# GpSimd multiplies two states by C in one operation, on another set of states

## The chip, the cores and the metric

The kernel runs on one core of one Trainium2 chip. The metric is the device time of one launch in microseconds. The engines are named as in the profile: PE is TensorE (matmuls), DVE is VectorE, ACT is ScalarE, POOL is GpSimd, SP is SyncE (it issues the DMAs here).

## What is computed

One transformer-like layer on x of shape 4 x 512 x 512 (four batches `b`, 512 steps of time, 512 features): a layer norm, then a selective state-space block and a gated feed-forward block on the same normed input, both added to x. What matters here is the state-space part, with 1024 channels and N = 16 states per channel:

```
dA  = exp(A * dt)                 # per channel, state and step
dBu = (dt * B) * hs
h   = dA_t * h + dBu_t            # a recurrence over the 512 steps
y   = sum over the 16 states of h * C_t
y   = (y + hs * D) * silu(gate)
out = y @ Wout^T
```

The feed-forward part is `gelu(x8 @ W0) * (x8 @ W1)`, rounded to fp8 and multiplied with a third matrix. It is cut into pieces and run beside the recurrence.

## The kernel before

Stage A (the first 220 us of the execution) norms the input, computes the projections and writes dt, dt * hs and hs of every unit to memory. Stage B, the rest, is what the change touches. It works through 32 **units**: for each batch `b` the eight blocks `k` = 0 to 7 of 128 channels. A tile is 128 channels by 512 steps, 512 fp32 numbers in a partition. In each unit, for each state n = 0 to 15:

- ACT makes `da` (line 994, `exp`) into one of four PSUM tiles (`SLOTS`), which it takes up again for state n + 4. It may do so when the state that lies there is left (`state_left`, line 803): for a state whose product is DVE's, when the product is made; for a state whose product is GpSimd's, already when the scan is done, because that scan wrote its result elsewhere.
- GpSimd makes `dbu` for two states at a time (line 833, 1024 numbers in a partition), into a ring of eight states (`DBUS`).
- DVE runs the recurrence as one scan (line 1095) from `da` and `dbu`. For a state of its own the result overwrites `da`, and DVE multiplies it by C (`times_c`, line 1070) behind the next state's scan, into a ring of eight. For a **pooled** state the result goes to the ring `hp` in SBUF, and GpSimd multiplies it by C there (line 1058).
- PE transposes each product into the sum of the unit (line 1222), states of DVE in step n, pooled state m in step m + `PE_LAG`, but at the latest in step 15.

Before the change the pooled states are 1, 4, 7, 9 and 12 in every unit, `hp` has five slots, and `PE_LAG` is 4. GpSimd's order is written out by hand (`body`, line 1042): in step n first `dbu` of states n and n + 1 if n is even, then the product of state n - 3 if that is pooled. Every wait is on its own engine's in-order queue, so an operation that waits holds all behind it.

Three further pieces lie in the loop. In the **feed-forward units** k = 1 to 5, ACT runs a gelu (line 972, with a table load on either side) between `da` of states 0 and 1, and DVE makes two bf16 operations (lines 1108 and 1111, together `act8`) behind the scan of state 4; GpSimd waits for their end before the product of the pooled state `PORT_GIVEN`. In every unit but the first, ACT copies the sum of the unit before (`y_t`, line 961) and makes its silu (line 982, again between two table loads) just before `da` of state 6 (`SWITCH`), and DVE multiplies the two (line 1078) behind the scan of state 7 (`GATED`). Units k = 0, 6 and 7 have no gelu and no `act8`; they are called the plain units below.

SP loads C and B of the next batch in unit k = 7, group by group, each when the products that read the old one are made.

Of the kernel before, what the change touches and what calls it, by code (L numbers as in the profile page):

```python
# [18 lines left out]
ALU = mybir.AluOpType  # L19
# [9 lines left out]
KU = DI // P  # L29
# [12 lines left out]
NS = 2  # L42
# [5 lines left out]
DTS = 4  # L48
SWITCH, GATED, GELU, SKIP = 6, 7, 1, 12
DBUS = 8  # L50
FIVE, FOUR = (1, 4, 7, 9, 12), (1, 4, 8, 12)
POOLED = (FIVE,) * KU
POOL_LAG, PE_LAG = 3, 4
HPS, PRODS = 5, 8
EARLY = 6


# [25 lines left out]

OWN = tuple(tuple(n for n in range(N) if n not in POOLED[k]) for k in range(KU))
PROD, HP = Ring(OWN, PRODS), Ring(POOLED, HPS)
ADDED = [{n: [m for m in POOLED[k] if min(m + PE_LAG, N - 1) == n] for n in range(N)} for k in range(KU)]

# [11 lines left out]
MADE = {group[:2]: k for k in OUT_A_LIN for group in OUT_A_LIN[k]}  # L99
OUT_A_COPIED = {(5, 8): 0, (5, 11): 1, (6, 8): 2, (6, 13): 3}  # L100
LIN_COPIED = {(5, 14): 0, (6, 1): 1, (6, 15): 2, (7, 14): 3}
GELU_USED, PORT_GIVEN = 4, 4
BACK = 4

MORE = {("out_a", 2): 5, ("out_a", 3): 6}
# [609 lines left out]
def stage_b(nc, xT, win_gate, wout, outT, ident, neg_a, skip, ahead, dram, sem, handed):  # L715
# [10 lines left out]
    with ExitStack() as ctx:  # L726
        def sb(name, shape, dt=F32):
            return ctx.enter_context(nc.sbuf_tensor(name, shape, dt))
# [7 lines left out]
        hp = sb("hp", [P, HPS, L])  # L736
# [4 lines left out]
        c_all = [c_head[:, g * NS:(g + 1) * NS, :] for g in range(G_AHEAD)]  # L741
# [32 lines left out]
        hp_ready, hp_used = sem("hp_ready"), sem("hp_used")  # L774
# [28 lines left out]
        def state_left(b, k, n):  # L803

            if n in POOLED[k]:
                return scanned, (b * KU + k) * N + n + 1
            return prod_ready, PROD.count(b, k, n)

        def unit_loads(b, k):

            return b * (16 * KU // 2) + 16 * (k // 2) + 16

        def run_units(eng, body):

            for k in range(HT):
                body(0, k, True)
            for b in range(B - 1):
                for k in range(HT, KU):
                    body(b, k, False)
                for k in range(HT):  # L820
                    body(b + 1, k, False)
            for k in range(HT, KU):
                body(B - 1, k, False)
# [6 lines left out]
        def two_states(slot, n):  # L830

            twice = unit[:, slot, 1:2, :].broadcast_to([P, NS, L])
            return nc.gpsimd.tensor_tensor(dbu[:, n % DBUS:n % DBUS + NS, :], twice, b_all[n // NS], ALU.mult)  # L833
# [193 lines left out]
        def gpsimd_b(pool):  # L1027
            def make_dbu(b, k, n, opening):
                u = b * KU + k
                if n == 0:  # L1030
                    pool.wait_ge(unit_loaded[k % 2], unit_loads(b, k))
                if k == 0 and n % NS == 0:

                    if n >= G_AHEAD * NS:
                        pool.wait_ge(b_loaded[n // NS], b * 16 + 16)
                    elif not opening:
                        pool.wait_ge(b_loaded[n // NS], b * 16)
                if not (opening and k == 0 and n < DBUS):
                    pool.wait_ge(scanned, u * N + n + NS - DBUS)
                two_states(k % 2, n).then_inc(dbu_ready, NS)  # L1040

            def body(b, k, opening):
                u = b * KU + k
                for n in range(N):

                    if n % NS == 0 and not (opening and k == 0 and n < EARLY):
                        make_dbu(b, k, n, opening)
                    m = n - POOL_LAG
                    if m in POOLED[k]:

                        tile = hp[:, HP.slot(k, m), :]
                        if 1 <= k <= FFN_UNITS and m == PORT_GIVEN:
                            pool.wait_ge(act8_ready, b * FFN_UNITS + k)
                            pool.sem_inc(waited, 1)
                        pool.wait_ge(scanned, u * N + m + 1)
                        if k == 0 and (m % NS == 0 or m - 1 not in POOLED[k]):
                            pool.wait_ge(c_loaded[m // NS], b * 16 + 16)
                        nc.gpsimd.tensor_tensor(tile, tile, c_all[m // NS][:, m % NS, :], ALU.mult).then_inc(hp_ready, 1)  # L1058

            run_units(pool, body)  # L1060

        def vector_b(dve):
# [260 lines left out]
```

## Time and profile before

| | us |
|---|---|
| median of 3 runs | 1091.9 (1091.71 to 1093.25) |
| the profiled execution | 1091.34 |
| its span, first to last instruction | 1089.6 |
| PE, DVE, ACT, POOL busy | 921.8, 1028.2, 799.4, 892.0 |

The span is cut into groups of instructions by line and engine, each with its count, mean duration and the idle time of its engine just before it, and what ended that. A timeline gives single instructions with their start; where rows of a kind follow each other they are merged (x2). Durations of neighbours on DVE, ACT and POOL overlap by a little, so what one costs a full engine is read from the distance of two starts, called the pitch here.

### The profile page before, as it was taken

Reading aid. Unit: us, or ns where it says so; the run is one execution under the profiler, and the core shown is the slowest. Engines: PE = TensorE matmul, PEld = TensorE weight load, DVE = VectorE, ACT = ScalarE, POOL = GpSimd, SP = SyncE. Lnnn points to the kernel's source line nnn. Section 1 sums busy time; section 2 is a strip of 40 time slices with the busy share of each in tenths; the row PEclk is TensorE's granted clock in tenths of the full one; section 3 lists DMA queues with packets and bytes.
Section 4 is the critical chain, followed back from the end, with each engine's and each line's share of the span. In section 5 each row is a group of like instructions: output and inputs, shape, how many; then the busy total and the mean of one; then the engine's idle time right before and its main releaser. Section 6 shows DMA issues by size and latency. Waiting matters only on the chain.

```text
span 1089.6 us, 14626 instructions
## 1 busy us (share of the span) xinstructions
PE 921.8 (85%) x4328; PEld 568.2 (52%) x4328; DVE 1028.2 (94%) x1214; ACT 799.4 (73%) x1134; POOL 892.0 (82%) x496
## 2 busy tenths in 40 slices
PE   3988889777777997998889969987998798879998
PEld 3746566444444554555545545554555555545554
DVE  7979898799999999999999999999999999999996
ACT  3777877677778665888886668888866688888662
POOL 4444525798888899988888999988889988888993
PEclk9999999979999999899899989999899899989999
DMA  8686878992111218342212183321212922212101
GB/s 280 197 273 226 308 209 326 370 371 86 54 59 37 69 61 282 143 144 70 67 33 84 56 305 122 128 78 59 82 45 75 343 90 92 78 59 78 39 0 39
DMA packets 53156, 150.23 MB, mean 138 GB/s; under 512 B 5728, under 2 KB 14048, under 8 KB 50016
## 3 DMA queue, kind: packets, MB, share of 16 engines
q1 hardware_dynamic: 53088, 149.41, 39.7%
q8 instruction: 32, 0.52, 0.2%
q14 instruction: 36, 0.29, 0.1%
HBM read 111.37 MB, written 38.01 MB: 137 GB/s over the span
## 4 chain that ended last, share of the span: by engine, by line
DVE 36%; issue 28%; ACT 17%; PE 13%; POOL 5%; DVEq 1%; DMA 1%; POOLq 0%
DVE da L1095 14%; DVE prod L1070 10%; DVE hp L1095 7%; ACT da L994 4%; PE yT L1222 3%; POOL dt_du L371 2%; ACT gate_bf L972 2%; PE mm L1131 2%; ACT L973 2%; ACT L972 2%; DVE y L1078 2%; ACT L983 2%; ACT L982 2%; POOL hs_lo L366 1%; DVE gate_bf L1108 1%
## 5 line engine op out<-in xcount | busy, mean ns | idle before, releaser
L994 ACT ACTIVATE da<-unit,neg_a 128x512 f32<-128x512 f32 x512 | 339.9, 684 | 201.8 <-DVE prod L1070 200.4
L833 POOL TENSOR_TENSOR dbu<-unit,b_head 128x1024 f32<-128x1024 f32 x192 | 449.0, 2362 | 0.0
L1095 DVE TENSOR_TENSOR_SCAN da<-da,dbu 128x512 f32<-128x512 f32 x352 | 418.0, 1219 | 1.3
L1222 PE MATMUL yT<-ident,prod 128*128 128x128 f32 x1408 | 228.8, 292 | 106.8 <-DVE prod L1070 106.4
L1222 PEld LDWEIGHTS yT<-ident,prod 128*128 128x128 f32 x1408 | 172.2, 148 | 235.1 <-DVE prod L1070 187.7
L1058 POOL TENSOR_TENSOR hp<-hp,c_head 128x512 f32<-128x512 f32 x128 | 162.9, 1273 | 67.2 <-DVE act L1111 62.4
L1095 DVE TENSOR_TENSOR_SCAN hp<-da,dbu 128x512 f32<-128x512 f32 x160 | 193.7, 1211 | 9.5 <-ACT da L994 9.5
L1070 DVE TENSOR_TENSOR prod<-da,c_head 128x512 f32<-128x512 f32 x256 | 171.7, 671 | 0.0
L1171 PE MATMUL mm<-xn_b,w_sb 128*128 128x512 fp8e4 x512 | 145.9, 417 | 8.2 <-ACT gate_bf L1004 6.6
L833 POOL TENSOR_TENSOR dbu<-unit,b_all 128x1024 f32<-128x1024 f32 x64 | 151.1, 2362 | 0.0
L1183 PE MATMUL mm<-xnT_b,wgate 128*128 128x512 f32 x256 | 130.3, 607 | 2.2 <-ACT gate_bf L1004 2.1
L1131 PE MATMUL mm<-y,wout_sb 128*128 128x512 f32 x242 | 114.6, 593 | 0.8 <-DVE y L1078 0.8
L1222 PE MATMUL yT<-ident,hp 128*128 128x128 f32 x640 | 100.8, 282 | 0.0
L366 POOL TENSOR_TENSOR hs_lo<-hs,hs_hi 128x512 fp32r<-128x512 f32 x32 | 44.7, 1401 | 60.3 <-ACT hs_hi L552 60.3
L1171 PEld LDWEIGHTS mm<-xn_b,w_sb 128*128 128x128 fp8e4 x512 | 51.3, 106 | 66.8 <-issue 37.2
L1222 PEld LDWEIGHTS yT<-ident,hp 128*128 128x128 f32 x640 | 79.0, 147 | 0.0
L432 DVE SCALAR_TENSOR_TENSOR conv<-proj,cols_sb,conv 128x511 f32<-128x511 f32 (+2 forms) x96 | 71.0, 747 | 4.6 <-ACT conv L534 2.4
L371 POOL TENSOR_TENSOR dt_du<-dt_du,hs 128x512 f32<-128x512 f32 x32 | 41.1, 1285 | 39.1 <-DVE dt_du L490 38.3
L599 PE MATMUL proj<-xnT_lo,win_hi 128*128 128x512 f32 x128 | 58.2, 455 | 9.3 <-issue 3.7
L1131 PEld LDWEIGHTS mm<-y,wout_sb 128*128 128x128 f32 x242 | 43.5, 191 | 42.9 <-issue 41.9
L1070 DVE TENSOR_TENSOR prod<-da,c_all 128x512 f32<-128x512 f32 x96 | 65.0, 678 | 0.0
L1192 PE MATMUL mm<-act,w_sb 128*128 128x512 fp8e4 x256 | 61.8, 379 | 0.0
(117 smaller groups left out, 1263.7 us busy)
## 6 DMA issues: line engine op xcount, KB each, us to landing
unit<-unit_d SPq DMA_DIRECT2D x32, 768.0 KB, 4.4
unit_d<-dt_du SPq DMA_DIRECT2D x32, 512.0 KB, 2.7
wf<-in_wffn SPq DMA_DIRECT2D x12, 1024.0 KB, 6.5
c_head<-bc_d SPq DMA_DIRECT2D x24, 512.0 KB, 5.1
b_head<-bc_d SPq DMA_DIRECT2D x18, 512.0 KB, 5.3
unit_d<-hs SPq DMA_DIRECT2D x32, 256.0 KB, 6.6
w_sb<-w_d SPq DMA_DIRECT2D x64, 128.0 KB, 4.3
wgate<-in_win_gate SPq DMA_DIRECT2D x32, 256.0 KB, 2.7
```

The costliest lines, as they stand in the source:

```text
L371: nc.gpsimd.tensor_tensor(dt_du[:, k % DTS, 1, :], dt_du[:, k % DTS, 0, :], hs[:, k, :], ALU.mult).then_inc(du_ready, 1)
L432: ins = nc.vector.scalar_tensor_tensor(out=conv[:, k % 2, back:L], in0=proj[k % 3][:, 0:L - back], scalar=cols_sb[:, k, C_TAP + TAPS - 1 - ...
L833: return nc.gpsimd.tensor_tensor(dbu[:, n % DBUS:n % DBUS + NS, :], twice, b_all[n // NS], ALU.mult)
L994: nc.scalar.activation(da[n % SLOTS][:, :], unit[:, k % 2, 0, :], ACT.Exp, scale=neg_a[:, k, n:n + 1]).then_inc(da_ready, 1)
L1058: nc.gpsimd.tensor_tensor(tile, tile, c_all[m // NS][:, m % NS, :], ALU.mult).then_inc(hp_ready, 1)
L1070: nc.vector.tensor_tensor(prod[:, slot, :], da[n % SLOTS][:, :], c_all[n // NS][:, n % NS, :], ALU.mult).then_inc(prod_ready, 1)
L1095: nc.vector.tensor_tensor_scan(state, da[n % SLOTS][:, :], dbu[:, n % DBUS, :], 0.0, ALU.mult, ALU.add).then_inc(scanned, 1)
L1131: return nc.tensor.matmul(bank[:, :], wout_sb[:, c, h * P:(h + 1) * P], y2[:, c, :], start=(c == first), stop=(c == last))
L1171: ins = nc.tensor.matmul(bank[:, :], wffn[:, k % 2, j, f, s, :].bitcast(FP8), xn8[:, f, :].bitcast(FP8), start=(f == 0), stop=(f == HT - 1))
L1183: ins = nc.tensor.matmul(bank[:, :], wgate[:, k % 2, c * P:(c + 1) * P], xnT[:, c, :], start=(c == 0), stop=(c == 3))
L1192: ins = nc.tensor.matmul(bank[:, :], wlin[:, i, h * P:(h + 1) * P].bitcast(FP8), act8[:, i, :].bitcast(FP8), start=(i == 0), stop=(i == HI ...
L1222: ins = nc.tensor.matmul(yT[k % 2][:, t * P:(t + 1) * P], product[:, t * P:(t + 1) * P], ident[:, :], start=False, stop=last, is_transpose ...
```

## The change

The pooled states change from (1, 4, 7, 9, 12) in every unit to (2, 3, 6, 7, 10, 11) in units k = 0, 2, 4, 6, 7 and (2, 3, 10, 11) in units k = 1, 3, 5. GpSimd makes the product of a pair in one operation of 1024 numbers, when the scan of the second is done, in step 6, 10 and 14. `hp` has six slots, pooled states join the sum five steps later instead of four, and the wait for `act8` stands before the pair (2, 3).

```diff
-FIVE, FOUR = (1, 4, 7, 9, 12), (1, 4, 8, 12)
-POOLED = (FIVE,) * KU
-POOL_LAG, PE_LAG = 3, 4
-HPS, PRODS = 5, 8
+SIX, FOUR = (2, 3, 6, 7, 10, 11), (2, 3, 10, 11)
+POOLED = (SIX, FOUR, SIX, FOUR, SIX, FOUR, SIX, SIX)
+POOL_LAG, PE_LAG = 3, 5
+HPS, PRODS = 6, 8
...
-GELU_USED, PORT_GIVEN = 4, 4
+GELU_USED, PORT_GIVEN = 4, 3
...
                     m = n - POOL_LAG
-                    if m in POOLED[k]:
-
-                        tile = hp[:, HP.slot(k, m), :]
+                    if m in POOLED[k] and m % NS == NS - 1:
+
+                        slot = HP.slot(k, m - 1)
+                        tiles = hp[:, slot:slot + NS, :]
...
                         pool.wait_ge(scanned, u * N + m + 1)
-                        if k == 0 and (m % NS == 0 or m - 1 not in POOLED[k]):
+                        if k == 0:
                             pool.wait_ge(c_loaded[m // NS], b * 16 + 16)
-                        nc.gpsimd.tensor_tensor(tile, tile, c_all[m // NS][:, m % NS, :], ALU.mult).then_inc(hp_ready, 1)
+                        nc.gpsimd.tensor_tensor(tiles, tiles, c_all[m // NS], ALU.mult).then_inc(hp_ready, NS)
```

What it moves on GpSimd, in unit k = 2, from the product behind the wait for `act8` to the first `dbu` of unit k = 3. Before:

```order
L1058 TENSOR_TENSOR hp<-hp,c_head 128x512 [waits act8_ready,scanned]
L833 TENSOR_TENSOR dbu<-unit,b_head 128x1024 [waits scanned] x2
L1058 TENSOR_TENSOR hp<-hp,c_head 128x512 [waits scanned]
L833 TENSOR_TENSOR dbu<-unit,b_all6 128x1024 [waits scanned]
L1058 TENSOR_TENSOR hp<-hp,c_head 128x512 [waits scanned]
L833 TENSOR_TENSOR dbu<-unit,b_all7 128x1024 [waits scanned]
L1058 TENSOR_TENSOR hp<-hp,c_all6 128x512 [waits scanned]
L833 TENSOR_TENSOR dbu<-unit,b_head 128x1024 [waits scanned,unit_loaded1]
```

Now (`b_all6` is B of states 12 and 13, `b_all7` of 14 and 15):

```order
L1059 TENSOR_TENSOR hp<-hp,c_head 128x1024 [waits act8_ready,scanned]
L833 TENSOR_TENSOR dbu<-unit,b_head 128x1024 [waits scanned] x2
L1059 TENSOR_TENSOR hp<-hp,c_head 128x1024 [waits scanned]
L833 TENSOR_TENSOR dbu<-unit,b_all6 128x1024 [waits scanned]
L833 TENSOR_TENSOR dbu<-unit,b_all7 128x1024 [waits scanned]
L1059 TENSOR_TENSOR hp<-hp,c_head 128x1024 [waits scanned]
```

Four single products between the wait and the next unit's `dbu` have become three pairs, and two pairs instead of two singles stand ahead of `dbu` of states 12 and 13.

On ACT, in unit k = 7 (plain), from `da` of state 0 to `da` of state 8. Each row is an `exp`, its wait tells by what its PSUM tile comes free. Before:

```order
L994 ACTIVATE da0<-unit,neg_a 128x512 [waits scanned,unit_loaded1]
L994 ACTIVATE da1<-unit,neg_a 128x512 [waits prod_ready]
L994 ACTIVATE da2<-unit,neg_a 128x512 [waits prod_ready]
L994 ACTIVATE da3<-unit,neg_a 128x512 [waits prod_ready]
L994 ACTIVATE da0<-unit,neg_a 128x512 [waits prod_ready]
L994 ACTIVATE da1<-unit,neg_a 128x512 [waits scanned]
L961 ACTIVATE y_t<-yT0 128x512 [waits hp_used]
L982 ACT_TABLE_LOAD [waits y2_ready]
L982 ACTIVATE sg<-mm1 128x512 [waits gate_mm]
L983 ACT_TABLE_LOAD
L994 ACTIVATE da2<-unit,neg_a 128x512 [waits prod_ready]
```

Now:

```order
L994 ACTIVATE da<-unit,neg_a 128x512 [waits prod_ready,unit_loaded1]
L994 ACTIVATE da<-unit,neg_a 128x512 [waits prod_ready] x5
L961 ACTIVATE y_t<-yT 128x512 [waits hp_used]
L982 ACT_TABLE_LOAD [waits y2_ready]
L982 ACTIVATE sg<-mm 128x512 [waits gate_mm]
L983 ACT_TABLE_LOAD
L994 ACTIVATE da<-unit,neg_a 128x512 [waits scanned] x2
```

`da` of state 0 and of state 5 now wait for a product of DVE (states 12 and 1 are no longer pooled), and `da` of states 6 and 7 only for a scan.

## Rows read from the trace of the kernel before

**Rows 1.** The page: the span, and each engine's busy time and instructions

```profile
span 1089.6 us, 14626 instructions
PE 921.8 (85%) x4328; PEld 568.2 (52%) x4328; DVE 1028.2 (94%) x1214; ACT 799.4 (73%) x1134; POOL 892.0 (82%) x496
```

**Rows 2.** Groups by line: out<-in, count | busy, mean ns | idle before, releaser

```profile
L833 POOL TENSOR_TENSOR dbu<-unit,b_head 128x1024 f32<-128x1024 f32 x192 | 449.0, 2362 | 0.0
L1095 DVE TENSOR_TENSOR_SCAN da<-da,dbu 128x512 f32<-128x512 f32 x352 | 418.0, 1219 | 1.3
L1058 POOL TENSOR_TENSOR hp<-hp,c_head 128x512 f32<-128x512 f32 x128 | 162.9, 1273 | 67.2 <-DVE act L1111 62.4
L1070 DVE TENSOR_TENSOR prod<-da,c_head 128x512 f32<-128x512 f32 x256 | 171.7, 671 | 0.0
```

**Rows 3.** Waits of the whole span: who waited for whom, us, times, longest

```profile
ACT da L994 <- DVE prod L1070: 200.4, 217, 2.4
POOL hp L1058 <- DVE act L1111: 62.4, 20, 3.8
DVE hp L1095 <- ACT da L994: 9.5, 20, 0.8
```

**Rows 4.** Timeline of POOL, a feed-forward unit: start, us, line, count

```profile
524.22 1.26 POOL L1058 TENSOR_TENSOR hp<-hp,c_head 128x512 f32<-128x512 f32 x1 [2.81 <-DVE act L1111]
525.45 4.66 POOL L833 TENSOR_TENSOR dbu<-unit,b_head 128x1024 f32<-128x1024 f32 x2
530.06 1.27 POOL L1058 TENSOR_TENSOR hp<-hp,c_head 128x512 f32<-128x512 f32 x1
...
534.83 2.36 POOL L833 TENSOR_TENSOR dbu<-unit,b_all 128x1024 f32<-128x1024 f32 x1
537.15 1.27 POOL L1058 TENSOR_TENSOR hp<-hp,c_all 128x512 f32<-128x512 f32 x1
538.38 7.00 POOL L833 TENSOR_TENSOR dbu<-unit,b_head 128x1024 f32<-128x1024 f32 x3
```

**Rows 5.** Timeline of DVE, same unit: scans of states 5, 6, 12, 0

```profile
523.96 2.34 DVE L1095 TENSOR_TENSOR_SCAN da<-da,dbu 128x512 f32<-128x512 f32 x2
526.21 0.68 DVE L1070 TENSOR_TENSOR prod<-da,c_head 128x512 f32<-128x512 f32 x1
526.80 1.21 DVE L1095 TENSOR_TENSOR_SCAN hp<-da,dbu 128x512 f32<-128x512 f32 x1
...
528.50 0.68 DVE L1078 TENSOR_TENSOR y<-yT,sg 128x512 f32<-128x512 f32 x1
529.10 1.22 DVE L1095 TENSOR_TENSOR_SCAN da<-da,dbu 128x512 f32<-128x512 f32 x1
...
534.76 1.22 DVE L1095 TENSOR_TENSOR_SCAN hp<-da,dbu 128x512 f32<-128x512 f32 x1
...
541.02 1.22 DVE L1095 TENSOR_TENSOR_SCAN da<-da,dbu 128x512 f32<-128x512 f32 x1
```

**Rows 6.** Timeline of ACT, start of the feed-forward unit before: gelu ahead of state 1

```profile
510.19 0.68 ACT L994 ACTIVATE da<-unit,neg_a 128x512 f32<-128x512 f32 x1
510.89 1.28 ACT L972 ACT_TABLE_LOAD   x1
```

**Rows 7.** Timeline of DVE, the same stretch: product of 11, product of 15, scan of 1

```profile
508.38 0.67 DVE L1070 TENSOR_TENSOR prod<-da,c_head 128x512 f32<-128x512 f32 x1
...
514.64 0.68 DVE L1070 TENSOR_TENSOR prod<-da,c_all 128x512 f32<-128x512 f32 x1
515.71 1.22 DVE L1095 TENSOR_TENSOR_SCAN hp<-da,dbu 128x512 f32<-128x512 f32 x1 [0.39 <-ACT da L994]
```

**Rows 8.** Timeline of ACT, a plain unit: states 4 and 5, `y_t`, states 6 to 8

```profile
600.54 1.30 ACT L994 ACTIVATE da<-unit,neg_a 128x512 f32<-128x512 f32 x2 [1.02 <-DVE prod L1070]
601.78 0.57 ACT L961 ACTIVATE y_t<-yT 128x512 f32<-128x512 f32 x1
...
605.58 1.91 ACT L994 ACTIVATE da<-unit,neg_a 128x512 f32<-128x512 f32 x3
```

**Rows 9.** Timeline of DVE, the same plain unit: scan 1, scans 5 and 6, product of 5

```profile
598.71 1.22 DVE L1095 TENSOR_TENSOR_SCAN hp<-da,dbu 128x512 f32<-128x512 f32 x1
...
604.97 2.57 DVE L1095 TENSOR_TENSOR_SCAN da<-da,dbu 128x512 f32<-128x512 f32 x2
607.45 0.67 DVE L1070 TENSOR_TENSOR prod<-da,c_head 128x512 f32<-128x512 f32 x1
...
623.98 1.21 DVE L1095 TENSOR_TENSOR_SCAN hp<-da,dbu 128x512 f32<-128x512 f32 x1
```

## The prediction, made before the changed kernel was run

> **What bounds the kernel now.** I read four views: the busy shares, the groups by line, the waits, and then the timelines of the three engines that feed each other. The busy shares put DVE first with 94% of the span [rows 1]. The groups say that in stage B it is nearly without gaps: 1.3 us idle ahead of 352 scans, none ahead of its products [rows 2]. The waits complete it: ACT waits 200.4 us for DVE's products, so ACT is mostly early; GpSimd's one large wait, 62.4 us in 20 pieces, is for `act8` in the feed-forward units; and DVE itself waits 9.5 us, 20 times, for ACT [rows 3]. So an operation taken from DVE shortens the kernel, but only while `da` and `dbu` still arrive in time. How much room they have is what the change spends, and only the timelines show it.
>
> Pitches, from distances of starts: two scans take 526.21 - 523.96 = 2.25, so 1.125 each; a DVE product 526.80 - 526.21 = 0.59; the gated product 529.10 - 528.50 = 0.60 [rows 5]. On GpSimd two `dbu` take 530.06 - 525.45 = 4.61, so 2.31 each, and a single product 538.38 - 537.15 = 1.23 [rows 4].
>
> **Products moved off DVE.** Before, 5 pooled states in 32 units, 160. Now (5 x 6 + 3 x 4) x 4 = 168. DVE makes 8 products fewer: 8 x 0.59 = **-4.7 us**. This is all that the change can give directly.
>
> **The price of a pair on GpSimd.** The trace has none. Its nearest row is `dbu`, a product of the same 1024 numbers in a partition: pitch 2.31 [rows 4]. From above, two singles bound it: 2.46. From below, 1.23 for one half and 2.31 for both leave 1.08 per half, so 2.16 without any fixed part; a lower price would need a faster rate per number than either form shows. I take 2.31. GpSimd's products then cost 84 x 2.31 = 194 us against 160 x 1.23 = 197: almost nothing is saved there, while the work comes in lumps.
>
> **Lumps ahead of `dbu`, in the units k = 2 and 4.** Call A the start of scan 5, right behind `act8`. GpSimd starts again at A + 0.26 (524.22 against 523.96), and from there works without a gap [rows 4, 5]. Before, `dbu` of states 14, 15 ended at 534.83 + 2.36 = 537.19, and that of states 0, 1 of the next unit at 538.38 + 2.36 = 540.74, where the scan of 0 began at 541.02: only 0.28 to spare [rows 4, 5]. Now, with pair (2, 3), `dbu` 8, `dbu` 10 and pair (6, 7) ahead of it, `dbu` 12 starts at A + 0.26 + 4 x 2.31 = A + 9.50 and ends at A + 11.86. DVE has the same number of products in between as before, so it wants scan 12 at A + 10.80 (534.76) [rows 5]. With 0.04 for the signal it begins at A + 11.90: a stall of 1.10. `dbu` 0 of the next unit is the eighth operation: it ends at A + 0.26 + 7 x 2.31 + 2.36 = A + 18.79; DVE wants it at A + 17.06 (541.02), plus 1.10 already lost, 18.16, and gets it at 18.83: a further 0.67. Together 1.77 in 2 units of 4 batches, 8 x 1.77 = **+14.2 us**. With pairs at 2.46 three pairs add 0.45, so 2.22 and +17.8; at 2.16 it is 1.32 and +10.6.
>
> In the units k = 1, 3, 5 two pairs (4.62) replace five singles and DVE has two products more than in the others: `dbu` 12 ends at A + 9.55, `dbu` 0 after pair (10, 11) at about A + 16.9, before DVE wants them (A + 12 and A + 18.2). No stall. The wait for `act8` now stands one product earlier in the queue, with `dbu` 8 behind it as before; `dbu` 6 lies ahead of it in both.
>
> **Gelu ahead of state 1.** ACT makes `da` 0, then two table loads and the gelu, then `da` 1. From the start of `da` 0 to scan 1: 515.71 - 510.19 = 5.52 [rows 6, 7]. DVE would have begun scan 1 at 514.64 + 0.59 = 515.23, so it loses 0.48; in unit k = 5, whose gelu is longer by 0.43, 0.91. That is 4 x (4 x 0.48 + 0.91) = 11.3 us now, of which the waits show 9.5 as idle [rows 3]. `da` 0 used to wait for scan 12 only. Now state 12 is DVE's, and `da` 0 waits for its product, which ends 0.67 after its start; signal 0.04; so scan 1 cannot start before 0.67 + 0.04 + 5.52 = 6.23 after the start of product 12. DVE by itself takes 3 scans and 4 products, 5.74. The loss is 0.50 (k = 5: 0.93). Behind the units k = 2 and 4 the stall of 0.67 at scan 0 already covers it: nothing is left at k = 3, 0.26 at k = 5. After: 4 x (3 x 0.50 + 0.26) = 7.0, so **-4.3 us**.
>
> **`y_t` and silu ahead of state 6.** In a plain unit `da` 4 and 5 start at 600.54, right behind product 0, because state 1 is pooled and its tile is free. `y_t` follows at 601.78, `da` 6 at 605.58 [rows 8]. Scan 6 starts at 607.45 - 1.125 = 606.33, 0.75 after that; the pair of scans takes 2.57 where it takes 2.34 elsewhere, a loss of 0.23 [rows 5, 9]. Now `da` 5 waits for product 1. With s for the start of scan 1 (598.71 in the row [rows 9]), product 1 starts at s + 1.125 + 0.59 + 1.125 = s + 2.84 and ends at s + 3.51. `da` 5 starts at s + 3.55, `y_t` 0.62 later, `da` 6 another 3.80 later (605.58 - 601.78), scan 6 another 0.75 later: s + 8.72. DVE wants scan 6 after five scans and products 0, 1 and 4: s + 7.40. Loss 1.32 instead of 0.23, in 3 plain units of 4 batches less the very first unit, 11 x 1.09 = **+12.0 us**. In feed-forward units `act8` gives ACT 2 us more before scan 6, so nothing is lost there. With this wait in it, DVE takes 18.0 + 10 x 0.59 + 0.60 + 1.32 = 25.8 for a plain unit; GpSimd needs 11 x 2.31 = 25.4, so it stays just behind the cover and costs nothing more.
>
> **Edges.** In the first unit GpSimd comes late from stage A and there is no silu to slow DVE: working the chain as above from the first scan gives 1.1 of stalls, less the 0.5 of gelu that they cover, **+0.6**. At the end two pooled states join the sum behind product 15 instead of one, 4 transposes of some 0.11 more; but PE works through a backlog there. I take **+0.2** (0 to 0.4). The ring of six holds one unit's states, and PE empties it in the same unit: nothing. The C loads in k = 7 wait about 2 us longer for the pair (10, 11); their readers come 10 us later and more: nothing.
>
> **Sum.** -4.7 + 14.2 - 4.3 + 12.0 + 0.6 + 0.2 = +18.0 on the profiled execution's 1091.34 gives 1109.3. The median of the runs lies 0.56 above that execution: 1109.9, say **1110.0 us**. With a pair at 2.16 it is 1106, at 2.46 about 1114.
>
> **A rule against the change.** The groups show 1273 ns for a product on GpSimd and 671 on DVE [rows 2]. The Trainium skill, page GPSIMD Engine Reference, section Engine selection, says to keep elementwise work on VectorE, GpSimd being about twice as slow with two inputs; the trace agrees, with 1.9. By that rule alone the eight moved states would add 8 x 1.16 of GpSimd time, which the pairing gives back, and the sum would be near no change.
>
> **The rivals.** First, **the fine pieces of lateness are absorbed** and only the busy sum of the fullest engine counts: faster. The ring of `dbu` is eight states deep; if GpSimd were ahead by more than 1.8 us when it passes the wait for `act8`, neither lump would reach DVE, and if `y_t` were not behind `da` 5, nor would the other. That is -4.7 on 1091.9: 1087.2. It speaks for it that GpSimd waits 62.4 us [rows 3]; against it that this wait is for DVE itself, so it cannot be used to run ahead, and the order of ACT is fixed in the code. It decides at scan 12: if `dbu` 12 is there by A + 10.8, which needs pairs of at most 1.78.
>
> Second, **only ACT's wait comes**, GpSimd is in time: -4.7 + 12.0 + 0.7 (gelu lost in full again) + 0.2 = +8: 1100.
>
> Third, **only GpSimd's lumps come**. Without the loss at state 6 (1.32 each), the plain units are GpSimd's: 25.4 against DVE's 24.5, some 0.9 in each after a first 0.3, about 2.2 a batch. -4.7 + 14.2 - 4.3 - 2.5 + 8 + 0.8: 1103.
>
> Fourth, **GpSimd's operations become dearer** or run into DVE's two bf16 operations. In the rows GpSimd is idle while these run [rows 3]. Now `dbu` 6 of the next unit ends at A + 0.26 + 10 x 2.31 + 2.36 = A + 25.7, and line 1108 begins at about A + 26.2: 0.5 to spare. If they met, up to one `dbu` (2.36) in 8 units would be at stake: 1112 to 1129. The page Advanced Engine Details and Errata of the Trainium skill, section VectorE Performance Modes, says that the second SBUF port is shared and that GpSimd and 2-port DVE instructions block each other; no run here shows its price.
>
> **How the numbers follow.** Forecast as worked out (1105 to 1115) 0.69; only ACT 0.08; only GpSimd 0.07; dearer 0.09; absorbed 0.05; a loss and gain that cancel within 0.2% 0.02. The range from 1100 to 1116 takes in the forecast, most of the second and third and a little of the fourth, about 0.84. Faster by over 0.2% 0.05, within 0.2% (2.2 us, about what a measurement of this kernel can tell from no change) 0.02, slower 0.93.
>
> **What the profile after will show.** The pair's group, 84 long, mean near 2360 ns. DVE idle behind GpSimd's `dbu`, twice in each of 8 units, about 1.0 and 0.6; no such wait in the page now. DVE waits for `da` at scan 6 of 11 plain units, about 1.2 idle each; the waits for `da` at scan 1 in about 16 units, 0.4 each. DVE products 344, 5 us less busy. The prediction is wrong if `dbu` 12 is ready before scan 12 in units k = 2 and 4, or if `da` 6 is ready at s + 7.4 in plain units.

## The result and the profile after

The changed kernel takes **1113.4 us** (median of 4 runs, 1112.5 to 1114.7) against 1092.6 for the kernel before beside it: a ratio of 1.0191, with a 95% interval of 1.0178 to 1.0204. It is 20.9 us slower. The forecast was 1110.0, in a range of 1100 to 1116.

The profiled execution took 1114.72, with a span of 1112.9. Of the 23.3 us between the two spans, 2.1 lie in stage A, which the change does not touch (the first scan starts at 222.5 instead of 220.4; over the eight experiments below it lies between 220.6 and 222.7). Stage B is 21.2 us longer. Where the text below gives the time of stage B in a trace, it runs from the first scan to the end of the span.

The page of the changed kernel: the busy line answers to [rows 1], the groups to [rows 2].

```profile
span 1112.9 us, 14588 instructions
...
PE 918.3 (83%) x4318; PEld 565.7 (51%) x4328; DVE 1023.0 (92%) x1206; ACT 800.7 (72%) x1134; POOL 891.7 (80%) x420
...
L1096 DVE TENSOR_TENSOR_SCAN da<-da,dbu 128x512 f32<-128x512 f32 x344 | 411.9, 1214 | 20.9 <-POOL dbu L833 13.5
...
L1059 POOL TENSOR_TENSOR hp<-hp,c_head 128x1024 f32<-128x1024 f32 x84 | 198.1, 2358 | 89.4 <-DVE act L1112 78.5
L1096 DVE TENSOR_TENSOR_SCAN hp<-da,dbu 128x512 f32<-128x512 f32 x168 | 203.2, 1210 | 13.6 <-ACT da L994 13.6
```

DVE has less to do (1023.0 against 1028.2) and is idle more. Ahead of its scans it stood idle for 10.8 us before (1.3 + 9.5); now it is 20.9 + 13.6 = 34.5. GpSimd is as busy as before (891.7 against 892.0): the loss does not lie in how much it does, but in when. The waits say behind whom, and in how many places (who waited for whom, us in total, times, longest), as in [rows 3]:

```profile
ACT da L994 <- DVE prod L1071: 212.4, 233, 2.6
POOL hp L1059 <- DVE act L1112: 78.5, 20, 4.7
...
DVE hp L1096 <- ACT da L994: 13.6, 11, 1.2
DVE da L1096 <- POOL dbu L833: 13.5, 17, 1.1
...
DVE da L1096 <- ACT da L994: 7.1, 16, 1.1
```

The last three are the result. Eleven waits of 1.24 us for `da`: the plain units. Waits for GpSimd's `dbu`, which the kernel before did not have at all: 15 of the 17 come from the units k = 2 and 4 (one at scan 12, one at scan 0 of the unit behind), two from the first unit of all. And 16 waits for `da` ahead of a scan of DVE's own states: 15 are the gelu's (20 before), the sixteenth, of 1.14, is a lump of a unit k = 4 that the profile puts down to ACT.

How one of the lumps looks. DVE, then GpSimd, in a unit k = 2 (start, us, line; A, the start of scan 5, is 284.62), to be held against [rows 4, 5]:

```profile
284.62 1.22 DVE L1096 TENSOR_TENSOR_SCAN da<-da,dbu 128x512 f32<-128x512 f32 x1
...
296.67 2.35 DVE L1096 TENSOR_TENSOR_SCAN da<-da,dbu 128x512 f32<-128x512 f32 x2 [1.15 <-POOL dbu L833]
...
303.60 1.23 DVE L1096 TENSOR_TENSOR_SCAN da<-da,dbu 128x512 f32<-128x512 f32 x1 [0.58 <-POOL dbu L833]
```

```profile
284.94 2.35 POOL L1059 TENSOR_TENSOR hp<-hp,c_head 128x1024 f32<-128x1024 f32 x1 [4.65 <-DVE act L1112]
287.25 4.67 POOL L833 TENSOR_TENSOR dbu<-unit,b_head 128x1024 f32<-128x1024 f32 x2
291.88 2.38 POOL L1059 TENSOR_TENSOR hp<-hp,c_head 128x1024 f32<-128x1024 f32 x1
294.20 4.67 POOL L833 TENSOR_TENSOR dbu<-unit,b_all 128x1024 f32<-128x1024 f32 x2
298.84 2.35 POOL L1059 TENSOR_TENSOR hp<-hp,c_head 128x1024 f32<-128x1024 f32 x1
301.14 6.99 POOL L833 TENSOR_TENSOR dbu<-unit,b_head 128x1024 f32<-128x1024 f32 x3
```

From the end of the wait GpSimd runs without a gap. `dbu` of states 12 and 13 starts at 294.20 = A + 9.58 and ends 2.36 later, at 296.56; scan 12 starts at 296.67 = A + 12.05 instead of A + 10.8. The eighth operation, `dbu` of state 0, starts at 301.14, and scan 0 waits for it once more.

The plain unit, to be held against [rows 8, 9]: ACT, then DVE (scan 1 is at 635.63 = s):

```profile
639.17 0.69 ACT L994 ACTIVATE da<-unit,neg_a 128x512 f32<-128x512 f32 x1 [1.02 <-DVE prod L1071]
639.80 0.58 ACT L961 ACTIVATE y_t<-yT 128x512 f32<-128x512 f32 x1
```

```profile
635.63 1.22 DVE L1096 TENSOR_TENSOR_SCAN da<-da,dbu 128x512 f32<-128x512 f32 x1
...
638.48 0.66 DVE L1071 TENSOR_TENSOR prod<-da,c_head 128x512 f32<-128x512 f32 x1
...
644.33 1.22 DVE L1096 TENSOR_TENSOR_SCAN hp<-da,dbu 128x512 f32<-128x512 f32 x1 [1.24 <-ACT da L994]
```

`da` of state 5 starts behind product 1 (638.48 + 0.66), at s + 3.54; before it started together with `da` 4. `y_t` follows at s + 4.17, and scan 6 at s + 8.70.

### The profile page after: what moved, and what is told of

Read it like the earlier page. It is cut to its first block and busy times, and to the rows that moved or that the text cites. A ratio compares the mean times of both kernels' runs of the same rounds, so it can differ in the third digit from the quotient of the medians.

```text
span 1112.9 us, 14588 instructions
## 1 busy us (share of the span) xinstructions
PE 918.3 (83%) x4318; PEld 565.7 (51%) x4328; DVE 1023.0 (92%) x1206; ACT 800.7 (72%) x1134; POOL 891.7 (80%) x420
## 5 line engine op out<-in xcount | busy, mean ns | idle before, releaser
L994 ACT ACTIVATE da<-unit,neg_a 128x512 f32<-128x512 f32 x512 | 343.6, 686 | 214.4 <-DVE prod L1071 212.4
L1096 DVE TENSOR_TENSOR_SCAN da<-da,dbu 128x512 f32<-128x512 f32 x344 | 411.9, 1214 | 20.9 <-POOL dbu L833 13.5
L1223 PE MATMUL yT<-ident,prod 128*128 128x128 f32 x1376 | 225.6, 292 | 134.4 <-DVE prod L1071 133.6
L1223 PEld LDWEIGHTS yT<-ident,prod 128*128 128x128 f32 x1376 | 166.6, 149 | 271.3 <-DVE prod L1071 237.9
L1059 POOL TENSOR_TENSOR hp<-hp,c_head 128x1024 f32<-128x1024 f32 x84 | 198.1, 2358 | 89.4 <-DVE act L1112 78.5
L1096 DVE TENSOR_TENSOR_SCAN hp<-da,dbu 128x512 f32<-128x512 f32 x168 | 203.2, 1210 | 13.6 <-ACT da L994 13.6
L1172 PE MATMUL mm<-xn_b,w_sb 128*128 128x512 fp8e4 x512 | 143.6, 411 | 8.4 <-ACT gate_bf L1004 4.7
L1071 DVE TENSOR_TENSOR prod<-da,c_head 128x512 f32<-128x512 f32 x216 | 144.3, 668 | 0.0
L1223 PEld LDWEIGHTS yT<-ident,hp 128*128 128x128 f32 x672 | 81.6, 145 | 9.8 <-issue 4.2
L1071 DVE TENSOR_TENSOR prod<-da,c_all 128x512 f32<-128x512 f32 x128 | 85.8, 671 | 0.0
```

The source lines that it names most:

```text
L994: nc.scalar.activation(da[n % SLOTS][:, :], unit[:, k % 2, 0, :], ACT.Exp, scale=neg_a[:, k, n:n + 1]).then_inc(da_ready, 1)
L1059: nc.gpsimd.tensor_tensor(tiles, tiles, c_all[m // NS], ALU.mult).then_inc(hp_ready, NS)
L1071: nc.vector.tensor_tensor(prod[:, slot, :], da[n % SLOTS][:, :], c_all[n // NS][:, n % NS, :], ALU.mult).then_inc(prod_ready, 1)
L1096: nc.vector.tensor_tensor_scan(state, da[n % SLOTS][:, :], dbu[:, n % DBUS, :], 0.0, ALU.mult, ALU.add).then_inc(scanned, 1)
L1172: ins = nc.tensor.matmul(bank[:, :], wffn[:, k % 2, j, f, s, :].bitcast(FP8), xn8[:, f, :].bitcast(FP8), start=(f == 0), stop=(f == HT - 1))
L1223: ins = nc.tensor.matmul(yT[k % 2][:, t * P:(t + 1) * P], product[:, t * P:(t + 1) * P], ident[:, :], start=False, stop=last, is_transpose ...
```

## The experiments

All runs are compared with the kernel before on the same chip. The theory has two parts: (1) in the units k = 2 and 4 GpSimd has more work behind the wait for `act8` than DVE gives it time for; (2) in the plain units ACT's block of `y_t`, silu and two table loads (3.8 us) is held up by product 1.

**The silu two states later.** Changed kernel, with

```diff
-SWITCH, GATED, GELU, SKIP = 6, 7, 1, 12
+SWITCH, GATED, GELU, SKIP = 8, 7, 1, 12
```

> The changed kernel with one number altered: ACT copies y_t and makes the silu ahead of da of state 8 instead of state 6 (SWITCH 6 to 8). There the four states in front are 3 to 7, of which 6 and 7 find their tiles free by a scan alone. Theory (ACT's block of 3.8 us is held by product 1, which delays da 6): the 11 idles of 1.24 us ahead of scan 6 in plain units go, each worth 1.34, so -14.7; but that wait covered GpSimd, which needs 25.4 us for a plain unit with three pairs where DVE then needs 24.5, so DVE idles behind dbu there instead, about 2.2 us a batch, +8: 1106 to 1107 us. Rival A (GpSimd has room in plain units): 1098 to 1099. Rival B (ACT is late in general, the place of its block does not matter): 1113, with the idle time at another scan.

Measured: 1107.4 us (ratio 1.0140, 1.0123 to 1.0157), 6.0 faster than the changed kernel (6.9 in stage B of the two traces). The 11 idles of 1.24 ahead of scan 6 are gone, and DVE's wait for `dbu` has grown from 13.5 us in 17 places to 19.1 in 28:

```profile
DVE da L1096 <- POOL dbu L833: 19.1, 28, 1.1
...
DVE da L1096 <- ACT da L994: 5.6, 16, 0.5
```

A plain unit of this run, where GpSimd now sets the pace (DVE's scan of state 0, and GpSimd's `dbu` for it, which ends at 679.78 + 2.36 = 682.14):

```profile
682.25 1.23 DVE L1096 TENSOR_TENSOR_SCAN da<-da,dbu 128x512 f32<-128x512 f32 x1 [0.58 <-POOL dbu L833]
```

```profile
679.78 4.68 POOL L833 TENSOR_TENSOR dbu<-unit,b_head 128x1024 f32<-128x1024 f32 x2
```

Part (2) holds: the place of the block costs 11 x 1.34 = 14.7 us. Less than half of it came back. The larger part of the rest was cover for GpSimd, which in a unit with three pairs is itself slower than DVE: ten new idles behind `dbu` in and right behind the plain units, 3.9 us, and four of 0.25 at scan 12 of k = 7, where `dbu` and `da` come within 0.1 us of each other. A smaller part is the edit's own price, which I had not asked for: `y_t` two states later makes PE's sum late, and DVE stands idle for 0.53 ahead of the gated product in the four units k = 6. The other way, the new idles cover the gelu's waits of three units k = 1.

**The wait for `act8` one pair later.** Changed kernel, with

```diff
-GELU_USED, PORT_GIVEN = 4, 3
+GELU_USED, PORT_GIVEN = 4, 7
```

> The changed kernel with one number altered: GpSimd waits for act8 before the pair (6, 7) instead of (2, 3) (PORT_GIVEN 3 to 7). Units k = 1, 3, 5 have no such pair, so they have no wait. Pair (2, 3) can start when scan 3 is done, about 3.2 us earlier, while DVE makes its two bf16 operations. Theory (the stalls of 1.15 and 0.6 us behind dbu in k = 2 and 4 come of the work queued behind that wait): both go, -15.3, and the gelu wait that they covered at k = 3 and 5 comes back, +4.6: 1102 to 1104 us. Rival (sharing with DVE): DVE's two bf16 operations, 0.94 and 0.96 us now, grow in all 20 feed-forward units, by up to the rest of a GpSimd operation, 2.36: at 1 us each it eats the gain, at 2 us the kernel is slower than 1113.

Measured: 1169.7 us (ratio 1.0714, 1.0695 to 1.0734), 56 slower than the changed kernel. The waits behind `dbu` did go, from 13.5 us to 1.1. That does not test part (1), since DVE itself became 3.2 us slower in each of these units, which alone gives GpSimd time; the run with four pooled states below does. The rival came: each of the two operations stayed within its limit of 2.36, but both pay in every unit. The groups of the changed kernel, then of this run:

```profile
L1112 DVE TENSOR_SCALAR act<-gate_bf 128x1536 fp8e4<-128x1536 bf16 (+1 forms) x20 | 20.3, 1013 | 3.6 <-DVE gate_bf L1109 3.6
L1109 DVE TENSOR_TENSOR gate_bf<-gate_bf,up_bf 128x1536 bf16<-128x1536 bf16 (+1 forms) x20 | 19.8, 991 | 0.0
```

```profile
L1112 DVE TENSOR_SCALAR act<-gate_bf 128x1536 fp8e4<-128x1536 bf16 (+1 forms) x20 | 57.9, 2894 | 3.6 <-DVE gate_bf L1109 3.6
L1109 DVE TENSOR_TENSOR gate_bf<-gate_bf,up_bf 128x1536 bf16<-128x1536 bf16 (+1 forms) x20 | 46.8, 2342 | 0.0
```

The two bf16 operations grew by 37.6 + 27.0 = 64.6 us. DVE's fp32 products, one of whose inputs lies in PSUM, did not grow (666 ns against 668): in this trace the 274 that lie wholly beside a busy GpSimd take 667 ns, the 37 with GpSimd idle 662.

**Both edits.** Changed kernel, with `SWITCH` at 8 and `PORT_GIVEN` at 7.

> The two edits of e1 and e2 together: y_t and silu ahead of state 8, act8 wait before the pair (6, 7). If both causes are right and separate, the gains add: -6.7 and -10.7 on 1113.4, so about 1096 us, with DVE's idle time then behind dbu in the plain units and at gelu's da 1. If the bf16 operations of DVE suffer beside GpSimd, more by what e2 shows.

Measured: 1174.6 us (ratio 1.0762, 1.0740 to 1.0783). The 1096 that I expected were without the price that the run above shows; here the two operations grew by (61.6 - 19.8) + (52.5 - 20.3) = 74.0 us, which makes 1170. It has one thing more to show. In unit k = 1 of three batches line 1109 took 7.2 us (longest 7191 ns) instead of 0.94. DVE, then GpSimd:

```profile
485.46 7.17 DVE L1109 TENSOR_TENSOR gate_bf<-gate_bf,up_bf 128x1536 bf16<-128x1536 bf16 x1
492.80 0.96 DVE L1112 TENSOR_SCALAR act<-gate_bf 128x1536 fp8e4<-128x1536 bf16 x1 [0.16 <-DVE gate_bf L1109]
```

```profile
484.87 2.34 POOL L1059 TENSOR_TENSOR hp<-hp,c_head 128x1024 f32<-128x1024 f32 x1
487.18 4.64 POOL L833 TENSOR_TENSOR dbu<-unit,b_head 128x1024 f32<-128x1024 f32 x2
495.04 2.36 POOL L833 TENSOR_TENSOR dbu<-unit,b_all 128x1024 f32<-128x1024 f32 x1 [3.22 <-DVE da L1096]
```

DVE's operation, started in the middle of the pair, did not end when the pair ended, but 0.81 us after the last of three operations that GpSimd ran back to back (487.18 + 4.64 = 491.82). GpSimd was then idle itself, waiting for a scan of DVE. The operation behind it ran with GpSimd idle and took its plain 0.96.

**Each product by itself, in step m + 3.** Changed kernel, with

```diff
-                    if m in POOLED[k] and m % NS == NS - 1:
-
-                        slot = HP.slot(k, m - 1)
-                        tiles = hp[:, slot:slot + NS, :]
+                    if m in POOLED[k]:
+                        tile = hp[:, HP.slot(k, m), :]
...
-                        if k == 0:
+                        if k == 0 and m % NS == 0:
...
-                        nc.gpsimd.tensor_tensor(tiles, tiles, c_all[m // NS], ALU.mult).then_inc(hp_ready, NS)
+                        nc.gpsimd.tensor_tensor(tile, tile, c_all[m // NS][:, m % NS, :], ALU.mult).then_inc(hp_ready, 1)
```

> The changed kernel's sets of states, ring and lag, but each product by itself again (512 numbers, each as soon as its own scan is done, in step m + 3). Theory (what hurts in k = 2 and 4 is how much work stands behind the wait for act8, and a pair puts state 2's half there too): the product of state 2 now goes ahead of the wait, five singles of 1.23 stand behind it (6.15) where three pairs did (6.93), so the two stalls together shrink from 1.9 to 1.1 in 8 units: -6.5, though GpSimd's own work grows by 84 x 0.15 = 12.6 us. The 11 waits for da at scan 6 stay as they are. 1106 to 1108 us. Rival (the pairing is what pays, and the loss comes from the choice of states alone): slower than 1113, up to 1126 if all of the 12.6 us reaches DVE.

Measured: 1126.4 us (ratio 1.0312, 1.0294 to 1.0330). The expectation failed, though the part that it was about did not: DVE's wait for `dbu` fell from 13.5 to 7.2 us. The time is that of the rival named there, that the pairing is what pays, but not by its cause, as this run and the next show. I had not asked what else the product of state 2 is ahead of. It now stands before `dbu` of state 6, and pushes that into DVE's first bf16 operation:

```profile
L1107 DVE TENSOR_TENSOR gate_bf<-gate_bf,up_bf 128x1536 bf16<-128x1536 bf16 (+1 forms) x20 | 35.7, 1784 | 0.0
```

One instance, DVE and then GpSimd, whose `dbu` ends at 285.26:

```profile
284.36 1.72 DVE L1107 TENSOR_TENSOR gate_bf<-gate_bf,up_bf 128x1536 bf16<-128x1536 bf16 x1
```

```profile
282.92 2.34 POOL L833 TENSOR_TENSOR dbu<-unit,b_head 128x1024 f32<-128x1024 f32 x1
```

The operations lie beside each other for 0.9 us, and line 1107 takes 1.72 instead of its plain 0.94 (0.99 is the mean with the longer units k = 5). Over 20 units it is 35.7 - 19.8 = 15.9 us. With 6.3 less behind `dbu`, and 0.38 more in each of 11 plain units (26.16 us from scan 6 to scan 6 instead of 25.78), that makes 13.8; measured are 13.0 (12.3 in stage B of the traces).

**Two singles in the pair's place.** Changed kernel, with

```diff
-                        nc.gpsimd.tensor_tensor(tiles, tiles, c_all[m // NS], ALU.mult).then_inc(hp_ready, NS)
+                        for i in range(NS):
+                            tile = hp[:, slot + i, :]
+                            nc.gpsimd.tensor_tensor(tile, tile, c_all[m // NS][:, i, :], ALU.mult).then_inc(hp_ready, 1)
```

> The changed kernel with each pair made by two operations of 512 numbers at the same place of GpSimd's queue. It measures the pairing alone: 84 x (2 x 1.23 - 2.31) = 12.6 us more of GpSimd. Theory (in k = 2 and 4 all of GpSimd's work behind the act8 wait lies on DVE's path, in the plain units ACT's wait covers it to within 0.4 us): the two stalls grow by 3 x 0.15 = 0.45, 8 x 0.45 = 3.6, plus about 0.1 in each plain unit: 1117 to 1119 us. The bf16 operations of DVE stay at 0.99 and 1.01, as dbu of state 6 still ends before they begin, by 0.1 to 0.3 us. Rival 1 (they are hit): up to 16 us more, as with the singles in step m + 3. Rival 2 (a pair saves nothing): 1113.

Measured: 1117.5 us (ratio 1.0234, 1.0217 to 1.0251), 4.0 slower than the changed kernel. DVE's wait for `dbu` is 16.8 us, again in 17 places, and the bf16 operation stayed at 993 ns. So the pairing by itself is worth 3 to 4 us (4.0 between the medians, 3.0 in stage B of the traces), and what the previous run lost it did not lose by single operations but by their place.

**Four pooled states in every feed-forward unit.** Changed kernel, with

```diff
-POOLED = (SIX, FOUR, SIX, FOUR, SIX, FOUR, SIX, SIX)
+POOLED = (SIX, FOUR, FOUR, FOUR, FOUR, FOUR, SIX, SIX)
```

> The changed kernel with four pooled states (2, 3, 10, 11) in units k = 2 and 4 as well, so two pairs behind every act8 wait. Theory: the 16 stalls behind dbu in these units go, 8 x 1.91 = -15.3; DVE makes 16 products more, +9.4; the gelu wait comes back at k = 3 and 5, which those stalls covered, +0.56 and +0.69 in 4 batches each, +5.0. Sum -0.9: 1112.5 us, that is, no difference from the changed kernel although its second largest cause is gone. Rival (the stalls come of something else than the count of pairs): they stay, 1123 us.

Measured: 1114.4 us (ratio 1.0210, 1.0193 to 1.0228). The 16 lumps of these units are gone; no wait of DVE for `dbu` is left there. DVE's waits for ACT at scan 1 have come back (11.0 us in 19 places instead of 6.0 in 15), and the 16 products are paid: part (1) holds, and the loss has only changed its place, as expected. Stage B is as long as in the changed kernel, within 0.1 us; the 1.0 between the medians is within the spread of the runs.

**The kernel before without its wait for `act8`.** 

```diff
-GELU_USED, PORT_GIVEN = 4, 4
+GELU_USED, PORT_GIVEN = 4, 5
```

> The kernel before with GpSimd's wait for act8 left out (PORT_GIVEN to a state that is not pooled), nothing else. GpSimd then works through while DVE makes its two bf16 operations. e2 showed these at 2.34 and 2.89 us beside GpSimd instead of 0.99 and 1.01. Theory (DVE and GpSimd shut each other out in these forms): the same growth, about 3.2 us in each of 20 units, +64, less what GpSimd's head start saves: 1145 to 1158 us. Rival (it is the pairs of 1024 numbers that block DVE, and a single of 512 would cost half): +20 to +30, 1115 to 1120.

Measured: 1148.7 us (ratio 1.0519, 1.0501 to 1.0537), 56.4 more. Its two bf16 operations grew from 1002 and 1014 ns to 1717 and 2920:

```profile
L1111 DVE TENSOR_SCALAR act<-gate_bf 128x1536 fp8e4<-128x1536 bf16 (+1 forms) x20 | 58.4, 2920 | 3.2 <-DVE gate_bf L1108 3.2
L1108 DVE TENSOR_TENSOR gate_bf<-gate_bf,up_bf 128x1536 bf16<-128x1536 bf16 (+1 forms) x20 | 34.3, 1717 | 0.0
```

That is (34.3 + 58.4) - (20.0 + 20.3) = 52.4 us, nearly the whole loss; 2.6 in each unit, where 3.2 was expected. Here a single of 512 numbers runs when the first bf16 operation is issued, and that costs it 0.7 us; the second meets `dbu` and loses 1.9. So here the price is about the time to the end of the GpSimd operation that is under way (a single does cost the first operation about half of what a pair did, 0.7 against 1.35, as the rival had it, but the second meets `dbu`), and the wait for `act8`, 62.4 us of GpSimd's time, saves 56 us of the kernel's.

**The feed-forward copies one state earlier, in the kernel before.** 

```diff
-FFN, FFN_COPIED = (5, 5, 5, 5, 4), (10, 10, 10, 10, 8)
+FFN, FFN_COPIED = (5, 5, 5, 5, 4), (9, 9, 9, 9, 7)
```

> The kernel before with the feed-forward copies on ACT one state earlier (FFN_COPIED 10, 8 to 9, 7), so that none lies between da of state 15 and da of state 0 of the next unit. There the chain product 11, da 15, copy, da 0, gelu, da 1 ends 0.48 us too late for scan 1 (0.91 at k = 5), the only idle of DVE in 20 units. Theory (that chain is what costs): a copy is 0.5 us of ACT, so nothing is left in 16 units and 0.4 in 4: 11.3 - 1.7 = -9.6, and GpSimd, which had 0.3 to spare at dbu of state 0, still just holds: 1083 to 1085 us. Rival 1 (GpSimd is the next bound at once): the idle goes over to scans behind dbu, 1088 to 1092. Rival 2 (ACT waits for PE at the earlier place): slower than 1092.

Measured: **1084.9 us**, ratio 0.9933 (0.9913 to 0.9953). This beats both kernels, the one before by 0.7%. DVE's waits for ACT fell from 9.5 us in 20 places to four, all at k = 5:

```profile
DVE hp L1095 <- ACT da L994: 2.7, 4, 0.7
```

In ACT's timeline `da` of states 15 and 0 now lie side by side (507.61), and the gelu's first table load starts 1.3 us after the first of them:

```profile
507.61 1.30 ACT L994 ACTIVATE da<-unit,neg_a 128x512 f32<-128x512 f32 x2 [0.50 <-DVE prod L1070]
508.93 1.28 ACT L972 ACT_TABLE_LOAD   x1
```

The profiled execution shows no wait of DVE for `dbu`: GpSimd's 0.28 of room held. The gain is 7.3 us between the medians, where 9.6 were expected; in stage B of the traces it is 8.3. The idle that went is 9.5 - 2.7 = 6.8, and 16 places with 0.09 of overlap regained in each make it 8.3, so the 0.1 per place was right. What failed is k = 5: 0.69 of idle is left there, 0.78 with the overlap, where I had expected 0.4, and 4 x 0.35 = 1.4 are missing.

## Why the prediction was right

**Products moved off DVE, -4.7.** 512 scans less 168 pooled are 344 products, as said; the pitch is still 0.59.

**The pair's price.** 2358 ns and a pitch of 2.31 to 2.32 (287.25 - 284.94), the value taken. Two singles in its place cost 3.0 us more in the traces and 4.0 between the medians; my upper end said 3.6.

**GpSimd's lumps, +14.2.** Right in kind and place, and 0.15 too small in each unit: in all eight, scan 12 starts at A + 12.03 to 12.05 (forecast 11.90) and scan 0 at A + 18.98 to 19.00 (forecast 18.83), so the lateness of the first stall is simply carried on to the second. Two small terms make it: GpSimd starts 0.32 after A, not 0.26, and DVE starts 0.11 after `dbu` ends, not 0.04 (296.67 against 296.56). From A to scan 0 is 1.92 more than the 17.06 of before, 8 x 1.92 = 15.4. The idles in these units sum to 13.5, and the rest is about 0.09 per stall by which neighbours on DVE otherwise overlap, and one stall that is split (0.23 at scan 8, 0.83 at scan 12). Unit k = 4 of batch 2 has the same 1.14, put down to ACT by the profile.

**Gelu, -4.3.** The idle at scan 1 is 0.47 where the state is reached without a stall, 0.21 at k = 5 and nothing at k = 3, as worked out. With the overlap it is 0.56 instead of 0.50, and 0.30 instead of 0.26 at k = 5: 4 x (3 x 0.56 + 0.30) = 7.9 after, so -3.4. That the stalls at scan 0 hide this wait was right: it came back when they were taken away.

**Silu, +12.0.** The loss is 1.24 + 0.1 = 1.34 in 11 places, forecast 1.32; scan 6 at s + 8.70, forecast s + 8.72.

**Edges.** In the first unit the two stalls are 0.52 and 0.60, and with the overlap 1.3 instead of 1.1; less the gelu's 0.56 that is +0.7. At the end (times less 1000) the last gated product starts 104.22 - 98.44 = 5.78 us after the last two products instead of 80.86 - 75.52 = 5.34: 0.44, just over the upper end of what I gave. My reason was the wrong way round. PE does work through a backlog there, without a gap from the last products to the transposes of `y_t`, and for that very reason nothing hides the longer work: the transposes of the pooled states in it take 0.87 from start to start (eight of them, 1101.81 to 1102.68) where they took 0.44 (four, 1078.87 to 1079.31), and DVE's gated product waits for PE.

```profile
1098.44 1.26 DVE L1071 TENSOR_TENSOR prod<-da,c_all 128x512 f32<-128x512 f32 x2
1104.22 0.69 DVE L1079 TENSOR_TENSOR y<-yT,sg 128x512 f32<-128x512 f32 x1 [4.52 <-PE yT L1128]
```

**The sum.** -4.7 + 15.4 - 3.4 + 12.2 + 0.7 + 0.4 = +20.6. The terms belong to stage B, which is 21.2 longer in the traces; between the medians it is +20.9. The forecast of +18.0 was short by the small terms above, most of them less than 0.1 us and recurring in unit after unit. A further 0.7 of the 3.4 us between 1110.0 and 1113.4 is the base: I built on 1091.9, and the kernel before took 1092.6 beside the changed one. Of the 0.6 left in stage B, 0.36 is one pause of DVE between its two bf16 operations in unit k = 1 of batch 2 (0.53 instead of 0.16), which the kernel before does not have; its cause is open, and the rest has no place.

**The rivals.** Lateness absorbed by the ring of `dbu`: it is not, since GpSimd is held at the wait by DVE itself. The second, that GpSimd is in time, fell with the lumps. The third rival's core, that GpSimd sets the pace of the plain units once ACT's wait is gone, is what the run with the later silu shows. The fourth, dearer operations beside each other, did not come: `dbu` of state 6 ended at 305.77 + 4.67 = 310.44, and line 1109 began at 311.01, 0.57 to spare where 0.5 was forecast. But its price is real, and my range for it was an estimate of one GpSimd operation at most; the run with both edits shows a wait through three.

## What to carry to other kernels

Where two engines feed each other through in-order queues and both are nearly full, the sum of their busy times says little: take one fixed point (here the end of a wait), add up what is queued behind it on the one engine, and compare each product's end with the moment at which the other wants it. A state's product also decides when its buffer comes free, so choosing other states for another engine moves the waits of a third one (here `da` of state 5, behind which 3.8 us of ACT's work lie). Ask of each wait that is to go what it covers: of the 14.7 us of ACT's wait only 6.0 came back with the later silu, and most of the rest went behind GpSimd.

## What the runs showed of the hardware

DVE's two bf16 operations, one with two inputs in SBUF, one a bf16 to fp8 conversion with one, do not run beside GpSimd's products, which read SBUF. They end about 0.8 us after the GpSimd operation does (1.1 in k = 5, where they are longer), almost their whole own length of 0.94 to 0.96, whether they took 1.72, 2.28 or 7.17 us in all. GpSimd is held up too: `dbu`, 2.36 otherwise, took 3.06, and up to 3.33, in the run with the later `act8` wait. DVE's scans and its fp32 products, each with one input in PSUM, are not touched: in that run 1209 and 667 ns beside a busy GpSimd, 1206 and 662 with GpSimd idle (scans of pooled states, products). The Trainium skill, page SBUF — State Buffer, section SBUF: two separate sides, says this: the port pair that VectorE and GpSimd share is an exclusive lock, and whoever comes first keeps it for the whole instruction. The trace agrees with the lock; but in the run with both edits DVE's operation, started 1.75 us before the pair ended, still waited through the two GpSimd operations queued behind it, 4.6 us more, which the rule for one instruction does not give. In the other 17 feed-forward units of that run, and in the run with the later `act8` wait, it got in behind the pair. Why it did there and not here no run settles.
